# A recurrent attention and mixture-of-experts layer on one core: GpSimd scatters tokens into sorted rows, and the experts run after the fifth round

## The reference

```
xn = layernorm(x)                               # x: 8 x 1024 x 256, so N = 8192 tokens of D = 256
q, k, v = xn @ Wq + bq, xn @ Wk + bk, xn @ Wv + bv     # 4 heads of 256
scores over the 4 HEADS of a token, for q*cos, k*cos and q*sin, k*sin; softmax; out = attn @ v
s = rearranged(out) @ Wo + bo
scores = (xn @ router_w + router_b) / temp      # 8 experts
gates = sinkhorn(scores, 3 iterations); the two best of 8 and their gates for each token
all_out = (relu(xn @ wg[e]) * (xn @ wp[e])) @ wo[e]    # 256 -> 512 -> 256
g = silu(xn + sum of the two experts' outputs by their gates)
out = x + s * g
```

## Time and profile before

| | us |
|---|---|
| median of 3 timed runs | 1612.05 |
| lowest, highest | 1609.37, 1612.59 |
| span of the profiled execution | 1604.5 |
| PE busy (matmul) | 1536.4 (96%) |
| DVE, ACT, POOL busy | 974.2, 730.0, 794.2 |
| DMA moved | 251.22 MB, mean 157 GB/s |

### The profile page before, as it was taken

The page is one execution under the profiler, slowest core; times in us unless marked ns, Lnnn a source line. Parts: engine busy times, 40 slices in busy tenths (PEclk is TensorE's granted clock), DMA queues, the critical chain, the costliest instruction groups (busy, mean ns, idle before and its releaser), DMA issues.

```text
span 1604.5 us, 32706 instructions
## 1 busy us (share of the span) xinstructions
PE 1536.4 (96%) x11408; PEld 1169.5 (73%) x11408; DVE 974.2 (61%) x1880; ACT 730.0 (45%) x1205; POOL 794.2 (49%) x945
## 2 busy tenths in 40 slices
PE   5998899989999999999999999999999999999997
PEld 2545666668888888888888888866667766667773
DVE  7567989953333333333333333577888788888777
ACT  5775333413333333333333333545566565565552
POOL 4647588813333343433334433244565465844456
PEclk9999799989999999999999999999999999999999
DMA  9989842263223131222211141253565665455464
GB/s 328 396 331 323 297 157 90 71 253 143 89 99 132 54 132 54 98 87 94 88 57 54 57 158 57 86 172 134 172 202 172 217 211 185 160 169 176 153 211 145
DMA packets 162678, 251.22 MB, mean 157 GB/s; under 512 B 13928, under 2 KB 121248, under 8 KB 161376
## 3 DMA queue, kind: packets, MB, share of 16 engines
q1 hardware_dynamic: 147904, 211.47, 38.1%
q0 software_dynamic: 12960, 35.41, 6.6%
q10 hardware_dynamic: 1664, 2.26, 0.4%
HBM read 149.58 MB, written 99.50 MB: 155 GB/s over the span
## 4 chain that ended last, share of the span: by engine, by line
PE 88%; DVE 5%; DMA 4%; ACT 1%; issue 1%; POOL 0%; ACTq 0%; SPq 0%; DVEq 0%
PE ps L1143 21%; PE ps L1078 21%; PE ps L1089 13%; PE ps L1162 11%; PE ps L1025 7%; PE ps L1152 3%; DMA AUX<-xn_d,AUX 3%; PE ps L1046 2%; PE ps L1125 2%; PE ps L994 2%; PE ps L922 1%; PE ps L978 1%; PE ps L912 1%; DVE UN L1228 1%; DMA WR<-w_d 1%
## 5 line engine op out<-in xcount | busy, mean ns | idle before, releaser
L1143 PE MATMUL ps<-WR,FR 128*128 x1620 | 408.4, 401 | 5.7 <-issue 3.1
L1143 PEld LDWEIGHTS ps<-WR,FR 128*128 128x128 f32 x1620 | 296.6, 190 | 65.0 <-issue 7.6
L647 POOL DMA_INDIRECT y_d<-AUX x135 | 133.3, 987 | 366.8 <-ACT AUX L866 366.8
L1654 DVE TENSOR_TENSOR AUX<-AUX,ps 128x512 f32<-128x512 f32 x135 | 92.9, 688 | 347.3 <-ACT AUX L854 347.3
L815 ACT ACTIVATE WM<-ps,bcs,trig 128x512 f32<-128x512 f32 x256 | 252.1, 1016 | 89.8 <-PE ps L1078 83.0
L1594 DVE TENSOR_SCALAR WM<-ps,vec,trig 128x512 f32<-128x512 f32 x256 | 243.9, 993 | 62.3 <-ACT WM L815 61.6
L1089 PE MATMUL ps<-WM,XTJ 128*128 128x512 f32 x512 | 237.1, 600 | 0.0
L854 ACT ACTIVATE AUX<-ps 128x512 f32<-128x512 f32 x135 | 80.9, 599 | 323.7 <-PE ps L1143 323.7
L1078 PE MATMUL ps<-XH,WH 128*128 128x512 f32 x512 | 205.8, 402 | 4.9 <-issue 3.8
L1162 PE MATMUL ps<-WR,ABR 128*128 x1080 | 209.4, 292 | 0.0
L1078 PE MATMUL ps<-XH,WL 128*128 128x512 f32 x512 | 200.5, 392 | 0.0
(11 more groups left out here) (238 smaller groups left out, 2238.4 us busy)
## 6 DMA issues: line engine op xcount, KB each, us to landing
US<-u_d SPq DMA_DIRECT2D x63, 512.0 KB, 5.1
u_d<-UN SPq DMA_DIRECT2D x120, 256.0 KB, 2.0
WR<-w_d SPq DMA_DIRECT2D x8, 3072.0 KB, 10.8
AUX<-y_d SPq DMA_DIRECT2D x32, 512.0 KB, 5.5
WM<-in_L_attn_x_dram SPq DMA_DIRECT2D x16, 512.0 KB, 9.5
xn_d<-WM SPq DMA_DIRECT2D x32, 256.0 KB, 7.3
w_d<-USR SPq DMA_DIRECT2D x16, 512.0 KB, 4.5
AUX<-xn_d SPq DMA_DIRECT2D x16, 512.0 KB, 6.3
```

The source lines that it names most:

```text
L647: e.indirect_dma_start(y_d, bass.IndirectOffsetOnAxis(toks[:, m - 5:m - 4], 0), YS[:, (m - 5) % 2, :], None).then_inc(s_y[(m - 5) % 2], 16)
L1143: mm = e.matmul(b[:, :], x, WR[:, bass.ds(off[m] + (2048 * z + 1024 * a + 512 * k), 512)], start=(k == 0 and x is xh and z == 0), stop=(k ...
L1654: e.tensor_tensor(HS[:, m % 2, :], GR[:, :], mP[m % 2][:, :], ALU.mult).then_inc(s_h, 1)
```

## The change

It has five parts.

1. The one-hot lists, their 128 matmuls and `listed` are gone. Instead the place of each token is kept as an integer (`posi`), and GpSimd, in rounds 1 to 4, loads the tokens' rows (`load_rows`) and scatters them into sorted rows `xs_d` (`send_rows`): 128 indirect DMAs. Since an expert's last tile is not full, `xs_d` (NM * 128 rows, 17.7 MB) is first filled with zeros by one DMA that ACT issues in the prologue.
2. The weights are no longer split and stored ahead. Wq and Wk are split by GpSimd at its start instead of by DVE. An expert's three matrices are loaded raw and split by GpSimd straight into the three places of WR (`load_part`, `split_part`): the first expert's after all scatters and after the 24th group of matrix M of round 4, the others' during the experts.
3. In the expert stage SP loads tile m from `xs_d` and stores its result to `ys_d` with plain DMAs.
4. In the rounds after the experts GpSimd gathers the results by 8 indirect DMAs for a round (`collect`, `collect_e`), and ACT multiplies them by the gates (`weighted`, 8 of 128x256 for a round, at c = 4..7, and for an early round or the last at c = 9..12).
5. QE is 5 in place of 4: round 4 comes ahead of the experts and has its c = 16..23 first (`order`). The early rounds 0 to 3 are finished in rounds 6, 8, 10 and 12. The gates' permutation (`weigh`) carries the places too and lies in round 2, `experts` in round 1.

```diff
-QE = 4
+QE = 5
+QF = QE - 1
+        def order(q):
+            return [*range(16, 24), *range(16)] if q == QE - 1 else list(range(24))
...
@@ sync
+            def load_tile(m):
+                if m >= 2:
+                    e.wait_ge(s_gt, m - 1)
+                e.dma_start(XG[:, m % 2, :], xs_d[128 * m:128 * m + 128, :]).then_inc(s_g[m % 2], 16)
+            def store_tile(m):
+                e.wait_ge(s_ye, m + 1)
+                e.dma_start(ys_d[128 * m:128 * m + 128, :], YS[:, m % 2, :]).then_inc(s_y[m % 2], 16)
+            for m in range(NM + 4):
+                if m < NM:
+                    load_tile(m)
+                if m >= 4:
+                    store_tile(m - 4)
...
@@ gpsimd
+            def load_rows(b):
+                e.wait_ge(s_x[b], 48)
+                for a in range(2):
+                    e.dma_start(XS[:, b % 4, 2 * a:2 * a + 2, :], halves(b)[:, a, :, :]).then_inc(s_xl[b % 4], 16)
+            def send_rows(b):
+                e.wait_ge(s_xl[b % 4], 32 * (b // 4 + 1))
+                for i in range(4):
+                    for k in range(2):
+                        e.indirect_dma_start(xs_d, bass.IndirectOffsetOnAxis(posi[:, k, 4 * b + i:4 * b + i + 1], 0),
+                                             XS[:, b % 4, i, :], None).then_inc(s_sc4[b % 4], 16)
...
+            e.wait_ge(s_disp, 2)
+            e.wait_ge(s_zd, 16)
+            for b in range(3):
+                load_rows(b)
+            for b in range(NQ):
+                send_rows(b)
+                if b + 3 < NQ:
+                    if b >= 1:
+                        e.wait_ge(s_sc4[(b - 1) % 4], 128 * ((b - 1) // 4 + 1))
+                    load_rows(b + 3)
+                if b in (2, 6, 10):
+                    xtj(b // 4 + 2)
+            e.wait_ge(s_md, 16)
+            e.wait_ge(s_ch, at(QE - 1, 23))
+            e.wait_ge(s_eoff, 1)
+            load_part(0)
+            load_part(1)
+            split_part(0)
+            load_part(2)
+            split_part(1)
+            split_part(2)
+            e.wait_ge(s_s, 4 * QE)
+            for p in range(3, 9):
+                load_part(p)
+            for p in range(3, 3 * E):
+                split_part(p)
+                if p + 6 < 3 * E:
+                    load_part(p + 6)
...
+            collect(QF, s_yn)
+            for q in range(QE, NQ):
+                xtj(q)
+                if q in host:
+                    collect_e(host[q])
+                total(q - 1)
                 if q in host:
                     total(host[q])
...
+                finish(q - 1)
+                if q < NQ - 1:
+                    collect(q, s_yn)
+                if q == NQ - 2:
+                    e.wait_ge(s_eo, QF)
+                    collect(NQ - 1, s_yl)
...
@@ scalar, among the copies of the 18 groups of the prologue
+                if j == 2:
+                    e.wait_ge(s_zt, 1)
+                    e.dma_start(xs_d.rearrange("(p m) d -> p m d", p=128),
+                                AB[:, 0, 0:D][:, None, :].broadcast_to([128, NM, D])).then_inc(s_zd, 16)
...
+            def weighted(q, c):
+                y1, y2 = (cE1, cE2) if q < QF else cs(q)[0:2]
+                if c == 0:
+                    e.wait_ge(*((s_ye2, 128 * q + 128) if q < QF else
+                                (s_yn, 128 * (q - QF + 1)) if q < NQ - 1 else (s_yl, 128)))
+                for k, y in enumerate((y1, y2)):
+                    ins = e.activation(y[:, c, :], y[:, c, :], ACT.Copy, scale=GP[:, c, k, q:q + 1])
+                if c == 3:
+                    ins.then_inc(s_we if q < QF else s_wn, 1)
```

More of the change, by code:

```diff
@@ new lines, in _, with spent, split_part @@
+            regs = [e.alloc_register(f"tend{i}") for i in range(2)]
+            def spent(x):
+                r = regs[x % 2]
+                e.reg_load(r, tendi[0:1, x:x + 1])
+                e.wait_ge(s_dn, e.snap(r, min_val=1, max_val=NM))
+                ch(e.tensor_tensor(hold[:, 0:1], hold[:, 1:2], hold[:, 1:2], ALU.add))
+            def split_part(p):
+                x, part, b = p // 3, p % 3, ring[p]
+                if part == 0 and x >= 3:
+                    spent(x - 3)
+                e.wait_ge(s_rb[b], 16 * ring[:p + 1].count(b))
+                hi = place_e(x) + (0, 1024, 4096)[part]
+                lo = hi + (2048, 2048, 1024)[part]
+                pieces = range(0, 1024, 256)
+                for z in pieces:
+                    ins = e.tensor_copy(WR[:, hi + z:hi + z + 256], RB[b][:, z:z + 256])
+                ch(ins)
+                for z in pieces:
+                    ins = e.tensor_tensor(WR[:, lo + z:lo + z + 256], RB[b][:, z:z + 256],
+                                          WR[:, hi + z:hi + z + 256].bitcast(F32), ALU.subtract)
+                ins.then_inc(s_wl, 1)
+                e.wait_ge(s_wl, p + 1)
@@ new lines, in _ @@
+            e.wait_ge(s_qk, 64)
+            for i in range(4):
+                split(i)
+            e.wait_ge(s_rm, NT // 2)
+            e.memset(AB[:, 0, 0:D], 0.0).then_inc(s_zt, 1)
+            xtj(0)
+            xtj(1)
+            e.wait_ge(s_disp, 2)
[10 more added lines that the diff above has]
+                    xtj(b // 4 + 2)
@@ L1072, in segment @@
                     e.wait_ge(s_xtd, 2 * q + 2)
[L1073 to L1074 removed]
+                    for c in order(q):
+                        b = ring(q, c)
                         if c < 16:
```

536 lines of the change are left out of this document (161 added, 375 removed).

## The result

The changed kernel takes 1838.68 us (median of 4 runs, 1828.15 to 1853.49) against 1610.71 us (4 runs, 1608.22 to 1612.59) for the kernel before: 1.142 times as long, 95% interval 1.137 to 1.147. The forecast was 1720, range 1655 to 1790: the sign was right and the size too small by 119 us. In the profiled execution the span is 1826.2 us, 221.7 more than before.

| stretch | before, us | after, us | difference | forecast |
|---|---|---|---|---|
| start to the experts' first matmul | 348.3, and 47.1 for the round that was moved ahead: 395.4 | 434.9 | +39.5 | +81 |
| the experts | 348.3 to 1022.4: 674.1 | 434.9 to 1119.3: 684.4 | +10.3 | -14 |
| rounds 5 to 15 | 1069.4 to 1604.5: 535.1 | 1119.3 to 1826.2: 706.9 | +171.8 | +41 |

The account below looks back on a forecast made before the run. PE was taken as the bound (88% of the chain), so the change was judged by what it puts in PE's way: +36 +50 -20 +41 on the old span of 1604.5, giving 1712, predicted 1720 us, range 1655 to 1790.

Parts of the forecast that it names:

- The fill, +36: Prologue: issuing the zero fill holds ACT about 40 us, so round 0 starts at 148 instead of 111.8 us.
- an issuer whose queue is full is held at the pace of the transfer: Zero fill in the prologue: pace read from SP's loads, 1.30 us per 512 rows, giving ACT up to 44 us.
- the first rival: Prologue: the fill does not hold ACT, 36 us less, 1684 us; chance 0.15.
- The rule of the Trainium skill: Zero fill: starting a DMA takes only the sequencer's issue time, so the 36 us would be near nothing.
- GpSimd's chain, +50: Rounds 1 to 4: 160 DMAs at 1.30 us, XTJs, then first weights' loads and splits make the experts 50 us late.
- XTJ of round 4: Before round 4's first group: XTJ comes behind 88 scatters and 28 loads, at 399; PE waits 36 us.
- The experts, -20: Expert stage: 660 us against 679.8, a gain of 20; tiles 4.84 us apart, waits for tile loads priced at nothing.
- Rounds 5 to 15, +41: Eleven rounds behind the experts: 534.8 us become 576, by ACT's waits for GpSimd's gathers and its added weighings.
- The waits of ACT for gathers behind c = 9: Rounds 6, 8, 10 and 12: ACT stands 8.8 us for late gathers, costing 7 us a round, 28 in all.

Follow-up runs that it names:

- q2: Changed kernel with 112 of the 128 scatters left out, so most rows of the experts' tiles stay zero; 1775.66 us, ratio 1.099 to the kernel before.
- q4: Changed kernel, gathers of rounds 5 to 14 moved into c = 0 to 15, scatters kept out of the scores of rounds 1 to 3; 1717.85 us.
- r1: q4 with the early block's gathers moved into c = 16 to 23 of the round before; 1673.31 us, ratio 1.039 to the kernel before.
- r2: r1 with the loads of the rows to be scattered issued by SyncE in place of GpSimd; 1736.03 us, ratio 1.077 to the kernel before.
- t1: Changed kernel with one 0.40 us GpSimd copy behind each gather, nothing else moved; 1715.20 us, ratio 1.064 to the kernel before.

## Why the prediction was wrong

**The fill, +36: the step failed.** ACT in the changed kernel, round its issue of the fill:

```profile
80.37 0.58 ACT L738 ACTIVATE WM<-ps 128x512 f32<-128x512 f32 x1
81.69 0.58 ACTq L732 DMA_DIRECT2D xs_d<-AB  x1
82.31 0.60 ACT L738 ACTIVATE WM<-ps 128x512 f32<-128x512 f32 x1 [1.36 <-PE ps L959]
```

The issue of 17280 rows took 0.58 us and they landed 54.1 us later. The step "an issuer whose queue is full is held at the pace of the transfer" was carried from many DMAs to one large one. The time (83) was nearly right and the price was that of the first rival, which had 0.15. (A slip in the working costs nothing here: 33.8 us for 18 groups are 1.88 each and not 1.83.) The rule of the Trainium skill, DMA: Bandwidth & Descriptors, section Issuing engines are not separate DMA queues, holds here.

**GpSimd's chain, +50 (with the fill, +81 on the table's bounds; measured +39.5): right in its pace, wrong as the thing that decides.** s_disp came at 189 (without the 36 us, 198 was forecast), the scatters stand 1.26 to 1.30 apart (1.30), end at 399, and the first expert's weights are ready at 418.5, 19.5 later (20). A plain load costs GpSimd 0.76 us and not 1.30 (six of them):

```profile
189.19 4.57 POOL L487 DMA_DIRECT2D AUX<-xn_d  x6 [32.86 <-DVE AUX L1365]
...
398.03 0.96 POOL L494 DMA_INDIRECT xs_d<-AUX  x1 [0.31 <-issue]
398.98 0.76 POOL L502 DMA_DIRECT2D WM<-in_L_ffn_wg_dram  x1
...
415.68 2.82 POOL L530 TENSOR_TENSOR WR<-WM,WR 128x256 fp32r<-128x256 f32 x4
```

But PE was later than GpSimd: round 4's scores end at 430.8. XTJ of round 4, priced at a wait of 36 us, was no obstacle either. PE had lost its time to the scatters, in the scores of rounds 1 to 3 and in round 4; q2, which has hardly any scatters and so no such chain on GpSimd either, puts that at 52.5 us. With all scatters in place GpSimd's chain sets the start as soon as PE is held less: at 425.4 in q4 and 421.6 in r1, 2.4 and 1.2 us behind the last split. In both ACT is still held beside the unbroken scatters of round 4, and PE stands 20 us in front of that round's scores; I had taken these 20 us for GpSimd's chain when I made r2. In t1, where nothing is held, the start is 414.4, PE waits 10.0 us for the splits, and 6.4 us for XTJ of round 4. So by t1 the chain is worth some 19 us against the table's 395.4, and the hold the other 20.

**The experts, -20 (here -14): the term failed, +10.3.** The tiles stand 4.84 us apart as forecast, and loads (landing 2.2 us, stores 1.7) are waited for 5.7 us in all. What I left out are tiles that start late by 0.35 us or more (first matmul of L1100): 26 of them here, 8 before. All lateness over 4.84 sums to 25.9 us here and 15.6 before. Two are 4.6 and 2.1 us; most of the others are under 1 us. In front of L1100 PE stands 10.7 us by "issue", in 22 pieces (3.1 us in 5 before, L1143), and no run isolated their cause.

**Rounds 5 to 15, +41: the step failed.** The waits of ACT for gathers behind c = 9, 7 us in each of four rounds, did not come: from round 5 on ACT waits for a gather once, 7.9 us in round 5 (8 forecast). The scores had become so long that the other gathers were out in time. c = 0 to 15 of rounds 6, 8, 10 and 12 is 3 us longer (25 us against 22.1), and that goes with the clock. The rows of rounds 7 and 8:

```profile
1252.20:1274.90 22.70, 22.38 (x100) 18.20 (x98) 19.02 (x28) 19.35 (x27) 7.62 (x8) 1.00 0.44 140
...
1320.60:1345.40 24.80, 24.80 (x98) 20.24 (x98) 15.81 (x24) 20.15 (x32) 6.53 (x10) 0.88 0.00 0
```

PE is busy throughout in both, but round 8 begins at the lower clock that the scores of round 7 left behind: 5.9 us of it are at half speed, which is some 3 us of work. Where the scores are short, the waits are there: in t1, with its gathers 1.65 us apart, ACT waits 67.2 us for them, and these c = 0 to 15 take 31 to 33. What I did not see is that a burst takes instructions from the other engines: 148 us. I priced the gathers' place, beside the scores, at nothing, "there PE is busy 471.3 of 472.8 us", and took an indirect DMA for a cost of GpSimd alone. The old trace holds 270 of them, but one or two at a time in each 4.84 us, and beside PE's large matmuls.

That the sign came out right is in part luck: the largest piece of the slowdown is one that no term of the forecast had, and the fill and GpSimd's chain together came to 39.5 us in place of 81.
